# Causal attention with its projections split into float32r halves, tile shapes regrouped, and the normalised rows made one step ahead

## The reference, cut to what matters

```python
x = x + _L0_attn_ref(_layernorm(x, axis=-1), L0_attn_Wqkv, L0_attn_Wout)
...
qkv = x @ Wqkv.T
qkv = qkv.reshape(batch, seq_len, 3, H, D)
...
q = q * cos + rotate_half(q) * sin
k = k * cos + rotate_half(k) * sin
scores = jnp.einsum('bhqd,bhkd->bhqk', q, k) * scale
causal = jnp.arange(seq_len)[None, :] > jnp.arange(seq_len)[:, None]
scores = jnp.where(causal[None, None], -jnp.inf, scores)
attn = jax.nn.softmax(scores, axis=-1)
out = jnp.einsum('bhqk,bhkd->bhqd', attn, v)
...
return out @ Wout.T
```

## Time and profile before

| | before |
|---|---|
| median of three runs | 1569.88 us |
| profiled execution, span | 1564.6 us |
| causal attention in it, from the first h to the last x | 8.9 to 202 us |
| busy share of the span: PE, DVE, ACT, POOL | 95%, 68%, 62%, 46% |
| mean granted clock of TensorE over the span | 0.983 of 2.4 GHz |

### The profile page before, as it was taken

How to read it: one execution, slowest core, us unless ns; L and a number is a source line. 1 busy time by engine, 2 the same in 40 slices (tenths; PEclk the granted TensorE clock), 3 DMA queues, 4 the chain that set the end, 5 groups by cost and what they waited for, 6 DMA issues and landing times. The chain is left out here.

```text
span 1564.6 us, 30305 instructions
## 1 busy us (share of the span) xinstructions
PE 1485.5 (95%) x10256; PEld 1212.1 (77%) x10256; DVE 1068.3 (68%) x2475; ACT 965.8 (62%) x2612; POOL 727.0 (46%) x891
## 2 busy tenths in 40 slices
PE   5999979999999999899997999899999999989998
PEld 2666668888888888788874555489999999967887
DVE  4676657888888887655545777655566665588887
ACT  2667647777777777533325877577777777742222
POOL 3666625555555555233333433213444444447675
PEclk8999989999999999999997999999999999999999
DMA  6000020000000000000003000020000000000000
GB/s 246 2 1 1 2 97 5 3 5 3 5 3 4 3 3 2 22 1 1 1 5 130 2 2 1 15 92 8 8 8 8 1 8 5 1 1 14 11 15 17
DMA packets 15609, 29.82 MB, mean 19 GB/s; under 512 B 1505, under 2 KB 12002, under 8 KB 14690
## 3 DMA queue, kind: packets, MB, share of 16 engines
q1 hardware_dynamic: 15458, 27.89, 4.9%
HBM read 25.79 MB, written 2.10 MB: 18 GB/s over the span
## 5 line engine op out<-in xcount | busy, mean ns | idle before, releaser
L1453 POOL TENSOR_TENSOR weights_even<-weights_even,cross_reciprocal 128x512 f32<-128x512 f32 x64 | 66.6, 1041 | 201.9 <-DVE cross_reciprocal L1686 201.9
L934 POOL TENSOR_TENSOR cross_work<-cross_work,cross_reciprocal 128x512 f32<-128x512 f32 x64 | 66.6, 1040 | 174.6 <-DVE cross_reciprocal L1091 174.6
L1535 ACT ACTIVATE weights_even<-bank,cross_shift 128x128 f32<-128x128 f32 x256 | 90.5, 366 | 79.1 <-DVE cross_shift L1678 79.1
L1157 PE MATMUL bank<-ident,cross_work 128*128 128x128 f32 x768 | 117.6, 276 | 2.5 <-DVE cross_work L1069 2.2
L987 ACT ACTIVATE cross_work<-bank,cross_shift,cross_q_rms 128x128 f32<-128x128 f32 x256 | 113.6, 455 | 5.2 <-DVE cross_shift L1063 4.0
L1157 PEld LDWEIGHTS bank<-ident,cross_work 128*128 128x128 f32 x768 | 90.2, 141 | 30.0 <-DVE cross_work L1069 21.1
L2481 DVE TENSOR_REDUCE grouped_maxima<-bank 128x4 bf16<-128x512 f32 x128 | 82.3, 684 | 35.9 <-PE bank L2564 35.9
L1962 POOL TENSOR_TENSOR mlp_low_inner<-mlp_inner,mlp_high_inner 128x512 fp32r<-128x512 f32 x36 | 48.7, 1353 | 116.4 <-ACT mlp_high_inner L2005 116.4
L1676 DVE TENSOR_REDUCE cross_maxima<-bank 128x4 f32<-128x512 f32 x64 | 44.1, 690 | 84.6 <-PE bank L1818 84.6
L404 POOL TENSOR_TENSOR causal_masked_maxima<-causal_maxima,causal_constants 128x512 bf16<-128x512 bf16 x64 | 67.0, 1068 | 56.6 <-DVE causal_maxima L549 56.6
L2830 ACT ACTIVATE mx_silu<-bank 128x512 f32<-128x512 f32 x32 | 19.1, 598 | 113.4 <-PE bank L2980 113.3
(11 more groups left out here) (375 smaller groups left out, 5292.6 us busy)
## 6 DMA issues: line engine op xcount, KB each, us to landing
weights_even<-in_weights SPq DMA_DIRECT2D x2, 2560.0 KB, 11.8
weights_even<-in_weights SPq DMA_DIRECT2D x2, 1732.0 KB, 8.6
weights_odd_early<-in_weights SPq DMA_DIRECT2D x1, 3072.0 KB, 11.9
weights_odd_values<-in_weights SPq DMA_DIRECT2D x1, 3072.0 KB, 18.9
weights_odd_late<-in_weights SPq DMA_DIRECT2D x2, 1536.0 KB, 9.4
x<-in_x SPq DMA_DIRECT2D x4, 512.0 KB, 8.2
out<-mx_result SPq DMA_DIRECT2D x16, 128.0 KB, 1.7
weights_even<-in_weights SPq DMA_DIRECT2D x2, 512.0 KB, 5.8
```

Of the source, the lines that this page charges most:

```text
L934: pool.tensor_tensor(probs[x], probs[x], reciprocal[x][:, :].unsqueeze(2).to_broadcast([P, PER, P]), ALU.mult).then_inc(probs_divided, 1)
L1157: last = pe.transpose(bank[:, j * P:(j + 1) * P], source, core.ident[:, :])
L1453: pool.tensor_tensor(probs[x], probs[x], reciprocal[x][:, :].unsqueeze(2).to_broadcast([P, JOBS, P]), ALU.mult).then_inc(probs_divided, 1)
L1535: last = act.activation(probs[x][:, j, :], bank_scores[x][:, j * P:(j + 1) * P], ACT.Exp, scale=SCALE, bias=shift[x][:, j:j + 1], accum_ou ...
```

## The change

- The four projections (queries and keys, values, output) take both operands as two float32r halves, high and low, and form three products: high x high, high x low, low x high. The layer's own weights are split at its start: ACT copies them in four pieces of 512 columns into float32r, DVE subtracts.
- The transposes of h of batch t+2 and of the heads of batch t-2, which lie side by side in one bank, are copied by one instruction of ACT (`copy_turned`), and DVE subtracts to get the low half (`low_turned`); PE waits for that (`turned_low`) ahead of the values.
- DVE normalises h of batch t+3 at the middle of step t, where it normalised t+2 at the start; the layer norm statistics of the chunks of four batches come one step later.
- PE subtracts the maxima ahead of the scores of the other pair, where it did so between the scores and the transposed scores, so groups of 128 rows and of 32 rows stand together; the transposed scores of the first pair move from the start of step t to the end of step t-1.
- ACT takes the exponentials of the second pair ahead of the second mask.
- The next part's weights: ACT makes the high half by a copy at the end of its step, POOL the low half by one subtraction at its old place. DVE's masking and POOL's second subtraction are gone.

```diff
 # POOL
-            def split_weights(b, s):
...
+            def take_low(b):
                 pool.wait_ge(weights_high, b + 1)
...
+                pool.tensor_tensor(slice_of(low_weights, b), slice_of(to_split, b),
+                                   slice_of(high_weights, b).bitcast(F32), ALU.subtract).then_inc(weights_low, 1)
             def step(t, s):
                 if batch_there(t):
                     mask_maxima(t, s, 1)
                 if batch_there(t):
-                    split_weights(t, s)
+                    take_low(t)
                 if batch_there(t + 1):
                     mask_maxima(t + 1, 1 - s, 0)
 # ACT
+            for k in range(WEIGHT_JOBS):
+                columns = slice(512 * k, 512 * (k + 1))
+                act.activation(split[0][:, columns], raw[:, columns], ACT.Copy).then_inc(own_high, 1)
+            def copy_turned(t, s):
...
+                act.activation(turned[s][0][:, turned_in(t)], bank_h[:, turned_in(t)], ACT.Copy)\
+                   .then_inc(turned_high, 1)
+            def take_high(b):
+                if b == 0:
+                    act.wait_ge(core.weights_loaded[n + 1], 16 * WEIGHT_PARTS)
+                act.activation(slice_of(high_weights, b), slice_of(to_split, b), ACT.Copy).then_inc(weights_high, 1)
             def step(t, s):
+                if batch_there(t + 2) or batch_there(t - 2):
+                    copy_turned(t, s)
...
                 if batch_there(t + 1):
                     copy_keys_and_own_queries(t + 1, 1 - s)
+                if batch_there(t):
+                    exponentials(t, 1)
                 if batch_there(t + 1) and not begins(t + 1):
                     lay_mask(t + 1, 1)
                 if batch_there(t):
-                    exponentials(t, 1)
+                    take_high(t)
 # DVE
+            def low_turned(t, s):
+                dve.wait_ge(turned_high, turned_by(t))
+                dve.tensor_tensor(turned[s][1][:, turned_in(t)], bank_h[:, turned_in(t)],
+                                  turned[s][0][:, turned_in(t)].bitcast(F32), ALU.subtract).then_inc(turned_low, 1)
             def step(t, s):
-                if batch_there(t + 2):
-                    layer.dve_normalise(dve, t + 2)
                 if batch_there(t + 1):
                     add_turned(t + 1)
+                if batch_there(t + 2) or batch_there(t - 2):
+                    low_turned(t, s)
                 if batch_there(t):
                     row_maxima(t, s, 1)
-                    take_high(t, s)
...
+                if batch_there(t + 3):
...
+                    layer.dve_normalise(dve, t + 3)
 # PE
+            def three_products(out, inputs, weights):
+                for c in range(EC):
+                    for x, y in PARTS:
+                        last = pe.matmul(out, inputs[x][:, c, :], weights[y][:, c, :],
+                                         start=(c == 0 and (x, y) == PARTS[0]),
+                                         stop=(c == EC - 1 and (x, y) == PARTS[-1]))
+                return last
             def step(t, s):
-                if batch_there(t):
-                    scores_transposed(t, s, 0)
...
+                if batch_there(t + 2) or batch_there(t - 2):
+                    pe.wait_ge(turned_low, turned_by(t))
...
+                if batch_there(t):
+                    subtract_maxima(t, 1)
                 if batch_there(t + 1):
                     scores(t + 1, 1 - s, 0)
...
                 if batch_there(t + 1):
+                    subtract_maxima(t + 1, 0)
                     scores(t + 1, 1 - s, 1)
+                    scores_transposed(t + 1, 1 - s, 0)
```

More of the change, by code:

```diff
@@ L315, in place @@
             return part.rearrange(pattern, **sizes) if pattern else part
-        wqk = place(EC * 2 * EMBED, "p (c n) -> p c n", c=EC)
-        wv, wo = (place(EC * EMBED, "p (c n) -> p c n", c=EC) for k in range(2))
+        WEIGHT_JOBS = EC * 4 * EMBED // 512
+        raw = place(EC * 4 * EMBED)
+        split = [sbuf(f"{name}_weights", [P, EC * 4 * EMBED], F32R) for name in ("high", "low")]
+        wqk = [w[:, 0:EC * 2 * EMBED].rearrange("p (c n) -> p c n", c=EC) for w in split]
+        wv, wo = ([w[:, k * EC * EMBED:(k + 1) * EC * EMBED].rearrange("p (c n) -> p c n", c=EC) for w in split]
+                  for k in (2, 3))
         constants = sbuf("constants", [P, dram["causal_constants"].shape[1]])
@@ L325, in causal_attention @@
         qk_cos, qk_sin, qk = (place(2 * EMBED) for k in range(3))
-        hT = [layer.hT, place(EC * P, "p (c t) -> p c t", c=EC)]
+        turned = [[sbuf(f"{name}_turned{s}", [P, 2 * EMBED], F32R) for name in ("high", "low")] for s in range(2)]
+        hT = [[half[:, 0:EMBED].rearrange("p (c t) -> p c t", c=EC) for half in turned[s]] for s in range(2)]
+        headsT = [[half[:, EMBED:2 * EMBED].rearrange("p (c t) -> p c t", c=EC) for half in turned[s]]
+                  for s in range(2)]
         qT_bf = [sbuf(f"qT_bf{s}", [P, EC, P], BF16) for s in range(2)]
@@ L360, in chunk_at_end_of, with turned_in, turned_by @@
         def chunk_at_end_of(t):
-            return t + 3 if isinstance(t, int) and t + 3 in range(1, CHUNKS) else None
+            return t + 2 if t + 2 in range(1, CHUNKS) else None
         def begins(b):
             return isinstance(b, int) and b < 2
+        def turned_in(t):
+            return slice(0 if batch_there(t + 2) else EMBED, 2 * EMBED if batch_there(t - 2) else EMBED)
+        def turned_by(t):
+            return t + 3
         def slice_of(tensor, b):
@@ L570, in statistics @@
                 layer.dve_statistics(dve, b, tail_step)
[L572 to L577, removed]
+            def low_turned(t, s):
+                dve.wait_ge(turned_high, turned_by(t))
+                dve.tensor_tensor(turned[s][1][:, turned_in(t)], bank_h[:, turned_in(t)],
+                                  turned[s][0][:, turned_in(t)].bitcast(F32), ALU.subtract).then_inc(turned_low, 1)
+            layer.dve_normalise(dve, 0)
+            for k in range(WEIGHT_JOBS):
+                columns = slice(512 * k, 512 * (k + 1))
+                dve.wait_ge(own_high, k + 1)
+                dve.tensor_tensor(split[1][:, columns], raw[:, columns], split[0][:, columns].bitcast(F32),
+                                  ALU.subtract).then_inc(own_low, 1)
             def step(t, s):
[L580 to L581 removed]
                 if batch_there(t + 1):
                     add_turned(t + 1)
+                if batch_there(t + 2) or batch_there(t - 2):
+                    low_turned(t, s)
                 if batch_there(t):
                     row_maxima(t, s, 1)
[L586 removed]
                 if batch_there(t - 2):
@@ L633, in scores, with subtract_maxima @@
                             last.then_inc(scores_filled, 1)
-            def scores_transposed(b, s, pair):
+            def subtract_maxima(b, pair):
                 for j in range(2):
@@ L671, in turn @@
                 last.then_inc(filled, 1)
-            def project_values(b, s):
-                pe.wait_ge(layer.hT_ready, b + 1)
-                for c in range(EC):
-                    last = pe.matmul(bank_h[:, 0:EMBED], hT[s][:, c, :], wv[:, c, :],
-                                     start=(c == 0), stop=(c == EC - 1))
-                last.then_inc(v_filled, 1)
-            def project_heads(b):
-                pe.wait_ge(headsT_ready, b + 1)
-                for c in range(EC):
-                    last = pe.matmul(bank_qk[:, 0:EMBED], headsT[:, c, :], wo[:, c, :],
-                                     start=(c == 0), stop=(c == EC - 1))
-                last.then_inc(layer.y_filled, 1)
+            def three_products(out, inputs, weights):
[5 more added lines that the diff above has]
+                return last
@@ L689, in project_queries_and_keys @@
                 pe.wait_ge(qk_read, nonneg(b))
-                for c in range(EC):
-                    last = pe.matmul(bank_qk[:, :], hT[s][:, c, :], wqk[:, c, :], start=(c == 0), stop=(c == EC - 1))
-                last.then_inc(qk_filled, 1)
+                three_products(bank_qk[:, :], hT[s], wqk).then_inc(qk_filled, 1)
             def step(t, s):
-                if batch_there(t):
-                    scores_transposed(t, s, 0)
-                if batch_there(t):
-                    pe.wait_ge(v_ready, t + 1)
```

71 lines of the change are left out of this document (30 added, 41 removed).

## The result

The changed kernel takes **1643.99 us** (median of 4 runs, 1643.75 to 1647.06), the kernel before beside it 1568.43 (1560.91 to 1570.82): a ratio of 1.0501 on record, 95% interval 1.0471 to 1.053 (the two medians by themselves give 1.0482). The predicted 1642 us, the direction and the place hold. The profiled span is 1642.0 us.

The account below looks back on a forecast made before the run. PE's own work was taken to bound the causal attention at 10.5 us a step. 13 steps x 4.9 = 63.7, with later steps, start and end 71.8, gave a span of 1636.4; plus 5.3, 1642 us; range 1612 to 1667.

Parts of the forecast that it names:

- The mechanism: Causal attention: POOL's low half waits for ACT's late high-half copy, delaying the masked maxima PE needs; POOL idle 4 to 5 us a step.
- The ring: Causal attention: six dependent links from masked maxima to the next step's, 14.2 us at full clock, 15.4 with the clock, against 10.5.
- The clock: PE in the causal layer: half-clock spells in most steps after longer idle stretches, adding 1.2 us a step.
- link 1: PE from masked maxima through subtraction, scores, transposed scores and transposes of h and heads: 2.1 us.
- link 4: PE's second half of subtracting, scores and transposed scores to their end: 1.6 us.
- link 6: POOL's low half 0.99 us, then two masked maxima 2.04 us: 3.1 us with the hand-over.
- the start: Start of the causal layer: splitting its own weights ahead of DVE's rotation delays it, 2 us charged.
- The step behind the steady ones: The step after the 13 steady ones, 9.1 us before, still has the wait: about 14 us, +5.
- The products: PE's projections: three float32r products for values, output, queries and keys save 0.8 us a step.
- The regrouping: PE's scores and subtraction: four changes of tile shape fewer a step save 0.4 us, up to 0.6.
- The ring at full clock: Rival: causal steps of 14.2 us without half-clock spells, 1625 us; chance 0.17, of which 0.05 near 1606.
- Half clock through most of the step: Rival: PE's links run at half clock, steps of 17.3 us, 1668 us; chance 0.11.

Follow-up runs that it names:

- run 1: The changed kernel with POOL's low half of the weights moved behind the next first pair's masked maxima: 1570.4 us, ratio 1.0044.
- run 2: The kernel before with only ACT's late high-half copy and POOL's one subtraction at its old place: 1636.93 us, ratio 1.0464.
- run 3: The changed kernel with unused matmuls, 11 and 3, filling PE's two waits: 1627.92 us, ratio 1.0387.
- run 4: The changed kernel with DVE's addition of the rotated halves held until POOL's two masks are done: 1633.53 us, ratio 1.043.
- run 7: run 1 plus DVE's second-pair row maxima before the low half, ACT's first exponentials before the mask, h(t+3) normalised earlier: 1554.62 us, again 1553.48.
- run 11: run 1 plus DVE's second-pair row maxima before the low half and ACT's second mask before the last two exponentials: 1566.97 us, ratio 1.0005.
- run 8: The kernel of run 7 with the four projections back in float32, without halves or own weight split: 1557.78 us, ratio 0.9955.

## Why the prediction was right

**The mechanism and its place** were right and are shown twice, by taking it out (run 1) and by putting it in alone (run 2). It was found by following program order: what stands behind a waiting instruction, and who needs that.

**The ring, link by link**, in one step of the changed kernel, from masks ready (133.17) to masks ready (149.43), with ACT's and POOL's timelines from which the middle is read:

```profile
137.05 0.60 ACT L455 ACTIVATE causal_high_turned<-bank 128x512 fp32r<-128x512 f32 x1 [7.39 <-PE bank L691]
...
139.60 1.12 ACT L489 ACTIVATE bank<-causal_constants 128x512 f32<-128x512 f32 x2 [0.58 <-DVE causal_maxima L563]
140.66 1.06 ACT L481 ACTIVATE weights_even<-bank 128x512 f32<-128x512 f32 x2
...
143.34 1.12 ACT L481 ACTIVATE weights_even<-bank 128x512 f32<-128x512 f32 x2
...
145.99 1.00 POOL L425 TENSOR_TENSOR low_weights<-weights_odd_early,high_weights 128x384 fp32r<-128x384 f32 x1 [4.90 <-ACT high_weights L508]
146.94 2.49 POOL L418 TENSOR_TENSOR causal_masked_maxima<-causal_maxima,causal_constants 128x512 bf16<-128x512 bf16 x2
```

| link | predicted us | measured us |
|---|---|---|
| 1 PE to the transposed heads | 2.1 and 1.2 for the clock | 3.88 (2.28 at full clock, run 3) |
| 2 ACT's copy, low half, maxima | 2.6 | 2.55 |
| 3 mask, first exponentials | 2.2 | 2.15 |
| 4 PE, second half | 1.6 | 1.59 |
| 5 exponentials, mask, high half | 2.6 | 2.65 |
| 6 low half, two masks | 3.1 | 3.44 |
| sum | 15.4 | 16.26 |

Three terms were sized too low. *The clock* took 1.6 us a step, not 1.2 (3.88 - 2.28), all in link 1, where every group runs at half speed. The prediction priced a spell that covers a part of links 1 and 4; what came covered, in a usual step, the whole of link 1 and left link 4 at the length priced for full clock. *Link 1 by itself* takes 2.28 us at full clock, not 2.1. That the clock would fall was read rightly from the earlier trace rows: it fell with gaps of 2.85 and 1.06 us that a burst of 0.2 us breaks up, and the windows above show it, 1.00 while PE stood idle and 0.50 once it had taken up work; with the gaps filled, two steps of three stayed at 1.00 (run 3). The Trainium skill ("TensorE: Matmul & The Clock Gate", section "Why this matters for your kernels") warns of one long gap between bursts. No wait of PE in the steady part was over 2.9 us, and the clock fell in every step all the same, so the measurement decides. *The masks* took 2.48 us, not 2.04, as the row of before had no addition beside them; that is the 0.34 in link 6. I priced the masks by a row taken alone, though the new ring puts them beside the addition. The Trainium skill names this neighbour: "GPSIMD Engine Reference", section "Specifications", has the engine's SBUF interfaces shared with VectorE and in contention with DVE instructions that have two SBUF inputs. The addition is one, and run 4 agrees, with 0.44 us.

**What cancelled.** That the time came within 2 us is luck: the mean step was 0.75 us longer than predicted (16.15 against 15.4), and the steps gave 73.4 instead of 63.7 us. Against these 9.7 us the start was 1.6 us early where I had charged 2, and the end took 0.06 where I had charged 0.6. DVE's rotation did begin later, as expected (15.86 us, 14.29 in the earlier trace rows). But the start ranged from 37.3 to 43.9 us over the profiled executions, 42.14 at a granted clock of 0.80 and 38.38 at 1.00 for one and the same kernel in run 7, so its 3.6 us are not the change's for certain. The rest, 3.3 us, is the way from span to median: I added 5.3, and the median is 2.0 over the profiled span. The step behind the steady ones (+4.9 for +5) and the last (+0.35 for +0.5) were right.

**The savings.** They existed, and the ring hid them. The products take 1.51 us for queries and keys (143.18 to 144.69 above) instead of 1.82, and values with output 1.64 (run 11) instead of 1.93: 0.6 us, for 0.8 predicted, since the first matmul of a group takes 0.22 to 0.34 us to the next instead of 0.12 to 0.23. The regrouping saves 0.3 us a half where nothing waits (1.62 in run 8, against 98.00 to 99.93 in the earlier trace rows), so 0.6 a step, the upper end of what I gave; part of it comes from something I had not foreseen, told below. With the ring undone a step could be 9.1 us by this (10.5 less 0.2 for the wait on h and twice 0.6), an estimate; PE's busy time in run 7 is 9.31 a step. The best measured is 9.8: in run 7 PE's weight loads still wait for DVE's low half and its rotated halves, 0.4 and 0.5 us a step.

**The rivals.** The ring at full clock would have been 14.2; run 3 has it at 14.66, which is 14.2 with 0.18 more in link 1 and 0.34 in link 6. Half clock through most of the step did not come: link 4 took 1.59, as priced for full clock. The forecast that run 1's step would reach PE's own work or 10.5 was not met: links 1 to 4 with the products behind them were priced at 10.5 in the prediction and came to 10.97.

## What to carry to other kernels

Moving an instruction to an engine with time to spare moves its *end* too: ask when its consumer comes in program order, and what stands queued behind that consumer; here two calls in the other order were worth some 71 us. Where rows are to price a new arrangement, check what will run beside each of them, and whether idle time ahead lowers the clock of what follows (here to 0.50 in link 1). A saving on the engine that seems full arrives only as far as the next ring lets it; measure the step, and not the busy time.

## What was not expected of the hardware

Scores and transposed scores use 32 rows of the array each. By the kernel, the scores of one pair and the transposed scores of the other lie in different rows. Put next to each other, such groups start together and overlap. PE's timeline of run 8:

```profile
107.04 0.61 PE L645 MATMUL bank<-minus_ident_bf,causal_masked_maxima 128*128 128x128 bf16 x8
107.58 0.28 PE L631 MATMUL bank<-causal_kT_bf,causal_qT_bf 32*128 32x256 bf16 x2
107.59 0.48 PE L656 MATMUL bank<-weights_even 32*128 32x256 f32 x2
107.70 0.27 PE L631 MATMUL bank<-causal_kT_bf,causal_qT_bf 32*128 32x256 bf16 x2
107.91 0.81 PE L656 MATMUL bank<-weights_even 32*128 32x256 f32 x6
108.66 0.44 PE L675 MATMUL bank<-ident,causal_h 128*128 128x128 f32 x2
```

The two groups start 0.01 us apart, and both are through in 1.08 us, from 107.58 to 108.66; one behind the other they took 0.32 + 1.06 in the earlier trace rows.

Two bf16 masks on POOL and a float32 addition on DVE, at the same time, cost each other 0.44 and 0.78 us (run 4), more together than POOL's whole subtraction of 0.99.
